# Rows normalised by GpSimd, one turn back, maxima turned by VectorE and an opening taken out of the loop, in a two-layer conditioned transformer

## The reference, cut to what matters

```
layer 0: sh_a,sc_a,gt_a,sh_m,sc_m,gt_m = split(silu(cond) @ Wada + bada)
  xm = (layernorm(x)*g1 + be1) * (1 + sc_a) + sh_a
  q,k,v = xm @ Wqkv;  P = softmax(causal(q @ k^T / 4))
  x = x + gt_a * ((P @ v) @ Wproj + bproj)
  xm = (layernorm(x)*g2 + be2) * (1 + sc_m) + sh_m
  x = x + gt_m * (gelu_exact(xm @ W1 + b1) @ W2 + b2)
layer 1: xm = layernorm(x) * (1 + scale1) + shift1        (scale, shift from cond)
  q,k,v = xm @ w^T + b;  P = softmax(q @ k^T / 4)          (no causal mask, a padding mask)
  x = x + (P @ v) @ wo^T + bo
  x = x + gelu_exact((layernorm(x)*(1+scale2)+shift2) @ w1^T + b1) @ w2^T + b2
```

## Time and profile before

| | before |
|---|---|
| runs, us | 1132.00, 1122.96, 1128.54 (median 1128.54) |
| the profiled execution, us | 1127.04 |
| its span, us | 1124.9 |
| PE, PEld | 1051.1 (93%), 905.2 (80%) |
| DVE | 828.6 (74%) |
| ACT | 592.0 (53%) |
| POOL | 347.9 (31%) |
| DMA packets | 50828, 81.46 MB |
| mean granted clock of TensorE | 0.968 |

### The profile page before, as it was taken

The page is one execution under the profiler, slowest core; times in us unless marked ns, Lnnn a source line. Parts: engine busy times, 40 slices in busy tenths (PEclk is TensorE's granted clock), DMA queues, the critical chain, the costliest instruction groups (busy, mean ns, idle before and its releaser), DMA issues.

```text
span 1124.9 us, 23896 instructions
## 1 busy us (share of the span) xinstructions
PE 1051.1 (93%) x8588; PEld 905.2 (80%) x8588; DVE 828.6 (74%) x2443; ACT 592.0 (53%) x1143; POOL 347.9 (31%) x333
## 2 busy tenths in 40 slices
PE   3879999999998899999998899999999888999998
PEld 3768888888886688998887787887888667889997
DVE  5478989999897476556638788898889845666553
ACT  1145666666665545433434677777777654344331
POOL 5112343343434544233411132323323343211111
PEclk9689999999999899999997899999999989999999
DMA  7565776757661020000068549466564400100001
GB/s 219 96 95 94 120 151 118 128 102 133 153 103 25 7 62 11 10 11 15 15 98 121 74 74 170 65 95 81 78 97 64 55 2 1 38 20 20 20 19 38
DMA packets 50828, 81.46 MB, mean 72 GB/s; under 512 B 8916, under 2 KB 23476, under 8 KB 49620
## 3 DMA queue, kind: packets, MB, share of 16 engines
q1 hardware_dynamic: 50232, 79.16, 40.3%
q10 hardware_dynamic: 480, 0.79, 0.6%
HBM read 22.64 MB, written 8.44 MB: 28 GB/s over the span
## 4 chain that ended last, share of the span: by engine, by line
PE 71%; DVE 8%; DMA 8%; SPq 5%; issue 4%; ACT 3%; POOL 1%; ACTq 0%; POOLq 0%; DVEq 0%
PE st_bank L576 14%; PE g_bank L576 12%; PE s_bank L576 8%; PE o_bank L576 8%; PE o_bank L664 7%; DMA k_stack<-qk_split 6%; SPq L433 4%; PE st_bank L643 3%; PE s_bank L626 3%; PE s_bank L630 3%; PE st_bank L649 3%; PE st_bank L645 2%; DVE maxima L1141 1%; PE g_bank L684 1%; PE st_bank L644 1%
## 5 line engine op out<-in xcount | busy, mean ns | idle before, releaser
L846 ACT ACTIVATE probs<-st_bank 128x384 f32<-128x384 f32 (+1 forms) x512 | 271.1, 545 | 194.1 <-PE st_bank L645 102.8
L1135 DVE CUSTOM_DVE_ANT_0 s_bank<-s_bank,tri_wide 128x128 f32<-128x128 f32 (+1 forms) x512 | 169.2, 382 | 25.6 <-PE s_bank L627 24.9
L1141 DVE TENSOR_REDUCE maxima<-s_bank 128x2 f32<-128x512 f32 x256 | 166.7, 675 | 24.7 <-PE s_bank L630 24.4
L933 ACT ACTIVATE probs<-st_bank,cols 128x512 f32<-128x512 f32 x112 | 77.2, 689 | 195.0 <-PE st_bank L576 185.1
L576 PE MATMUL st_bank<-qk_split,q_stack 128*128 128x512 f32 x696 | 166.5, 397 | 1.7 <-ACT probs L846 0.9
L576 PEld LDWEIGHTS st_bank<-qk_split,q_stack 128*128 128x128 f32 x696 | 129.3, 188 | 33.7 <-issue 1.9
L576 PE MATMUL g_bank<-xmT,wa 128*128 128x256 f32 x768 | 123.8, 301 | 4.8 <-POOL xmT L1358 4.8
L664 PE MATMUL o_bank<-probs,v_sb 128*32 128x256 f32 (+1 forms) x2048 | 126.1, 365 | 0.1
L630 PE MATMUL s_bank<-k_stack,q_stack 97*128 97x256 f32 x512 | 114.0, 307 | 12.2 <-DMA k_stack<-qk_split 6.9
L630 PEld LDWEIGHTS s_bank<-k_stack,q_stack 97*128 97x128 f32 x512 | 80.9, 196 | 41.1 <-issue 25.5
L649 PE MATMUL st_bank<-q_stack,k_stack 99*128 99x256 f32 x512 | 106.0, 291 | 6.6 <-ACT probs L846 3.3
(11 more groups left out here) (119 smaller groups left out, 2231.3 us busy)
## 6 DMA issues: line engine op xcount, KB each, us to landing
q_stack<-qk_split SPq DMA_DIRECT2D x192, 128.0 KB, 4.6
k_stack<-qk_split SPq DMA_DIRECT2D x186, 128.0 KB, 6.1
gate_rows<-gate_dram SPq DMA_DIRECT2D x32, 128.0 KB, 3.4
w_dram<-w_in SPq DMA_DIRECT2D x8, 512.0 KB, 7.2
wm_f32r<-w_dram SPq DMA_DIRECT2D x4, 1024.0 KB, 11.0
out<-x_sb SPq DMA_DIRECT2D x8, 512.0 KB, 2.9
x_sb<-x_in SPq DMA_DIRECT2D x4, 512.0 KB, 7.5
q_stack<-q_stack SPq DMA_DIRECT2D x4, 384.0 KB
```

The lines of the kernel that those rows point to most:

```text
L846: activation(probs[:, h % 8, 0:n], st_bank[h % 2][:, 0:n], ACT.Exp, scale=SCALE)\
L933: activation(h_of[b.const > 0][:, m % 2], h_bank(b, m)[:, :], ACT.Gelu, bias=cols[:, cb + m:cb + m + 1]).then_inc(m_gelu, 1)
L1135: last = v.tensor_tensor_reduce(out=bank[:, keys], in0=bank[:, keys], in1=tri_wide[:, T - (i + 1) * P:T], scale=1.0, scalar=LOWEST, op0=AL ...
L1141: v.reduce_max(maxima[:, gb.mod(2), :, slot], bank[:].rearrange("p (i n) -> p i n", n=T), AX.X).then_inc(max_done, 1)
```

## The change

1. From batch 2 of each layer on, in steady steps, POOL normalises the rows (two operations of 128x256) right after the inverse deviation; DVE did it at slot 9. DVE keeps the batches that open a layer.
2. The two scaling operations on DVE move from slots 0 and 7 to 4 and 8; the two turns back of 128x256 (slots 2, 8) become one of 128x512 at slot 9; ACT's high part of `attnT` moves from slot 9 to 10, the output projection from slots 12 and 14 to 13 and 15; POOL makes the low part in two operations of 128x256 where it was one of 128x512.
3. The turned maxima come from one DVE operation (a turn of 32x32 blocks over 128x64) at the end of the step that makes them. PE's two transposes, ACT's copy and their waits are gone. SP moves the maxima with four DMAs of 8 KB, whose pieces are 128 bytes, where it were two of 16 KB.
4. In layer 0, SP's wait for the added x and the load of the gate rows stand behind the restacks of q and k, where they stood ahead of both.
5. Layer 0's first two batches are opened ahead of the loop, which starts at t = 2. The block of conditioning matmuls is spread over the slots of step 2, one piece to a slot, behind that slot's scores; they go into `o_bank` instead of `s_bank[2]`. ACT issues the restack of k for the first two batches, not only for the first; v of batch 1 is made in step 2.

```diff
-SLOT = {"q": (0, 1), "negmaxT": 1, "k": (3, 5), "v": (6, 7), "xT": 12, "proj": (12, 14)}
-TURN, SCALED, TURN_BACK, ATTN_HIGH, PROJ_OUT = (14, 6), (0, 7), (2, 8), 9, 15
+SLOT = {"q": (0, 1), "k": (3, 5), "v": (6, 7), "xT": 12, "proj": (13, 15)}
+TURN, SCALED, TURN_BACK, ATTN_HIGH, PROJ_OUT = (14, 6), (4, 8), 9, 10, 15
-        negmaxT = sb("negmaxT", [32, T], f32r)
+        negmaxT = sb("negmaxT", [P, NT, 32])
...  (SP, step)
-                    when(negmaxT_copied, g.count(1, 1))
-                    for e in range(2):
-                        sp.dma_start(q_stack[ROW_MAX + e:ROW_MAX + e + 1, stack_of(g)].bitcast(fp32),
-                                     negmaxT[H * e:H * (e + 1)].bitcast(fp32)).then_inc(max_loaded[g.mod(2)], 16)
-                    if layer == 0:
-                        when(x_added, c.count(1, -1))
-                        load_gates(c, 0)
+                    when(negmax_turned, g.count(1, 1))
+                    rows = q_stack[ROW_MAX:ROW_MAX + 2, stack_of(g)].bitcast(fp32)\
+                        .rearrange("e s (i b n) -> e s i b n", i=NT, n=32)
+                    for blk in range(P // 32):
+                        sp.dma_start(rows[:, :, :, blk], negmaxT[32 * blk:32 * (blk + 1)])\
+                            .then_inc(max_loaded[g.mod(2)], 16)
...
+                if layer == 0 and c.within(B):
+                    if c.const == 0:
+                        store_tables()
+                    when(x_added, c.count(1, -1))
+                    load_gates(c, 0)
...  (PE, step)
-                    if s == SLOT["negmaxT"] and c.within(B):
-                        pe.wait_ge(negmax_ready, gc.count(1, 1))
-                        bank = take(layer, t, "negmaxT")
-                        for i in range(NT):
-                            src = negmax[:, gc.mod(2), i].bitcast(fp32).rearrange("p e s -> p (e s)")
-                            last = transpose(bank[0:32, i * P:(i + 1) * P], src, ident[:])
-                        last.then_inc(negmaxT_ready, 1)
...
+                    if layer == 0 and t.const == AHEAD and only is None:
+                        set_up(s)
...  (PE, the opening)
+            step(0, Step(0), "new")
+            pe.wait_ge(setup_done, 1)
+            step(0, Step(1), "project")
+            step(0, Step(1), "new")
+            step(0, Step(2), "project")
             for layer in range(LAYERS):
-                for t in steps(B, AHEAD * layer, 5):
+                for t in steps(B, AHEAD, 5):
                     step(layer, t)
-                    if layer == 0 and t.const == 1:
-                        set_up_columns()
-                        set_up_rows()
...  (DVE)
-                    if s == 9 and n.within(B):
-                        row_normalise(layer, n)
-                    if s in TURN_BACK and d.within(B):
-                        turn_back(gd, TURN_BACK.index(s))
+                    if s == TURN_BACK and d.within(B):
+                        turn_back(gd)
-                v.transpose(attnT_full[:, f], packed[:, f]).then_inc(attnT_ready, 1)
+                v.transpose(attnT_full.rearrange("p f n -> p (f n)"), packed[:].rearrange("p f n -> p (f n)"))\
+                    .then_inc(attnT_ready, 1)
...  (DVE, the end of negative_maximum)
+                v.transpose(negmaxT[:].rearrange("p i n -> p (i n)"),
+                            dst.bitcast(fp32).rearrange("p i e s -> p (i e s)")).then_inc(negmax_turned, 1)
...  (POOL)
-                g_.tensor_tensor(attnT[:, 1], attnT_full, attnT[:, 0], ALU.subtract).then_inc(attnT_lo, 1)
+                for f in range(NF):
+                    last = g_.tensor_tensor(attnT[:, 1, f], attnT_full[:, f], attnT[:, 0, f], ALU.subtract)
+                last.then_inc(attnT_lo, 1)
...
+            def row_normalise(layer, n):
+                gn = in_layer(layer, n)
+                wait(pool, xT_ready, gn.count(1, -1))
+                pool.wait_ge(rstd_ready, gn.count(1, 1))
+                rows = xrows(n, NT)
+                for i in range(NT):
+                    last = g_.tensor_scalar(xn[:, gn.mod(2), i], rows[:, i * D:(i + 1) * D], mv[:, gn.mod(2), i, 0:1],
+                                            rstd[:, gn.mod(2), i:i + 1], ALU.subtract, ALU.mult)
+                last.then_inc(xn_ready, 1)
+                if n.within(B) and t.const >= AHEAD:
+                    row_normalise(layer, n)
```

More of the change, by code:

```diff
@@ L341, in stack_of, with v_due @@
             return g.const % B % SBUFS
+        def v_due(layer, t, only):
+            if layer == 0 and t.const == AHEAD:
+                return only is None
+            return active(layer, t, only)[1].within(B)
         def active(layer, t, only):
@@ L350, in active @@
                 return off, a, off, off, off
-            if layer == 1 and t.const == AHEAD:
+            if t.const == AHEAD:
                 return n, off, b, c, d
@@ L704, in step @@
                                 last.then_inc(ready, 1)
-                    if s in SLOT["v"] and a.within(B):
+                    if s in SLOT["v"] and v_due(layer, t, only):
                         i = SLOT["v"].index(s)
+                        ga = in_layer(layer, t - 1)
                         if i == 0:
@@ L865, in step @@
                         exponentials(gc, s - LAG)
-                    if s == SLOT["negmaxT"] and c.within(B):
-                        act.wait_ge(negmaxT_ready, gc.count(1, 1))
-                        last_batch = gc - 1
-                        wait(act, max_loaded[last_batch.mod(2)], last_batch.half().count(32, 32)
-                             if c.const + layer else None)
-                        activation(negmaxT[:], g_bank[0][0:32, 0:T], ACT.Copy).then_inc(negmaxT_copied, 1)
                     if s == SLOT["q"][1] and a.within(B):
@@ L876, in step @@
                         high(k_ready, k_hi, k_stacked, g_bank[0], k_split, NF)
-                    if s == SLOT["k"][1] and a.within(B) and a.const + layer == 0:
+                    if s == SLOT["k"][1] and a.within(B) and layer == 0 and a.const < 2:
                         act.wait_ge(k_lo, ga.count(1, 1))
@@ L974, in mlp_step @@
                     step(1, Step(2), "project")
+            step(0, Step(0), "new")
+            step(0, Step(1), "project")
+            step(0, Step(1), "new")
+            step(0, Step(2), "project")
             for layer in range(LAYERS):
-                for t in steps(B, AHEAD * layer, 5):
+                for t in steps(B, AHEAD, 5):
                     if t.const == 3:
-                        act.wait_ge(setup_done, 3)
-                        act.wait_ge(mask_stored, 16)
                         wait(act, m_added, 2 * NCH * layer or None)
@@ L1119, in step @@
                 n, a, b, c, d = active(layer, t, only)
+                if layer == 0 and t.const == AHEAD:
+                    a = t - 1
                 gn, ga, gb, gc, gd = (in_layer(layer, s) for s in (n, a, b, c, d))
@@ L1191, in scale @@
                 dve.wait_ge(rsum_ready, g.count(NF, f + 1))
-                wait(dve, attnT_ready, g.count(NF, f - 1))
+                wait(dve, attnT_ready, g.count(1))
                 if g.const == 0:
@@ L1209, in negative_maximum @@
                 dve.wait_ge(max_done, g.count(H, H))
-                wait(dve, negmaxT_ready, g.count(1, -1))
+                wait(dve, negmax_turned, g.count(1))
                 v.tensor_scalar(dst[:, :, 0], m, -1.0, None, ALU.mult).then_inc(negmax_hi, 1)
@@ L1293, in _ @@
             for layer in range(LAYERS):
-                for t in steps(B, layer + 1, 5):
-                    if layer == 0 and t.const == 1:
-                        split_attention_weights()
+                if layer == 0:
+                    split_attention_weights()
+                    row_statistics(0, Step(1))
+                    row_normalise(0, Step(1))
+                    step(0, Step(1), "project")
+                    set_up_constants()
+                for t in steps(B, AHEAD, 5):
                     step(layer, t)
-                    if layer == 0 and t.const == 1:
+                    if layer == 0 and t.const == AHEAD:
                         set_up_columns()
@@ L1359, in modulated_low, with step @@
                     .then_inc(xmT_ready, 1)
-            def step(layer, t):
-                n, d = t, t - 4
+            def step(layer, t, only=None):
+                n, a, b, c, d = active(layer, t, only)
                 gd = in_layer(layer, d)
```

103 lines of the change are left out of this document (57 added, 46 removed).

## The result

The changed kernel takes 1163.4 us (median of four runs, 1158.54 to 1166.01) against 1128.35: ratio 1.031, interval 1.0273 to 1.0347. It is 3.1% slower where 1129, no change, was forecast, and outside the range (1106 to 1146).

The account below looks back on a forecast made before the run. PE was taken to bound the kernel (busy 49.02 of 50 us), DVE close behind. 1127.04 - 1.8 (opening) + 0.7 (layer 0 steps) - 1.1 (layer 1 steps) + 4.5 (last steps) = 1129.3, forecast 1129, range 1106 to 1146.

Parts of the forecast that it names:

- The DMAs of the maxima: Steady step: maxima split at 204.81, four DMAs issued by 207.5, landed at 209.2, before PE wants them at 209.80.
- The margin of 0.6 us: Maxima's DMAs land 0.6 us before PE's need, at 0.59 an issue; holds up to 0.75 us an issue.
- The slower rival: Maxima's DMAs come late at PE's first transposed scores of slot 4: 1.0 us in about 26 steps, 1155; chance 0.17.
- The projection: Steady steps: PE waits 0.67 (layer 0) or 0.61 (layer 1) for POOL's low part of attnT; 0.70 taken for both.
- The step without stalls: Distance between slot 12 transposes without stalls: 19.27 us before, less 0.22 for PE's two removed transposes.
- The first rival: Low part of attnT is in time: 24 steady steps lose 0.70 each, the tails 3; 1109.5; chance 0.32.
- The gate rows: Behind the restacks in layer 0: restacks begin up to 1 us sooner, so step-start stalls (0.45, 0.77) go.
- the forecast sign: In the changed profile, the stalls marked "issue" at the start of steps are gone.
- Normalising on POOL: DVE loses 2 x 0.775 us; POOL takes about 0.71 each, covered by its idle 5.04; worth nothing where PE bounds.
- The opening: Layer 0's start: step 2 ends at 61 to 63, gain 1.1; next three steps -0.7; -1.8 in all, bounds +3 and -10.
- The last steps: End of each layer: longer way to the low part costs +2.2 a layer, +4.5 in all, between 0 and 9.
- the prediction's own sign of having failed: Forecast fails if PE's steady-step waits sum to other than 0.7, or layers' last steps move over 5 us each.

Follow-up runs that it names:

- bias_waits: Changed kernel with one wait added: POOL's addition of the bias waits until both halves of the negated maxima are written; 1134.0 us, ratio 1.005.
- the pairs of the square: Four kernels compared: changed kernel 1163.4 us, maxima freed (bias_waits) 1134.0, projection freed (later_no_wait) 1141.1, both (projection_later) 1123.4.
- projection_later: bias_waits with scaling, turn back and high part of attnT one slot earlier (3 and 7, 8, 9), projection left at 13 and 15; 1123.4 us, ratio 0.9938.
- later_no_wait: projection_later without the wait of POOL's bias addition, so the changed kernel with scaling, turn back and high part a slot earlier; 1141.1 us, ratio 1.0119.
- opening_and_gates: Changed kernel with parts 1, 2 and 3 undone, leaving the opening ahead of the loop and gate rows behind the restacks; 1128.1 us, ratio 0.9982.
- earlier_and_waits: Changed kernel with scaling, turn back, high part and projection one slot earlier, and POOL's bias addition waiting for the negated maxima; 1125.3 us, ratio 0.9973.

## Why the prediction was wrong

- **The DMAs of the maxima**: this step failed, in its first term. "Split at 204.62 + 0.19" took the duration of the second maximum operation from the kernel before, where it began 0.26 ahead of POOL's addition. The change moved the projection to slot 15 and the two met. The operation took 1.27, so everything behind it was 1.1 late. bias_waits and the pairs of the square show it: 29 and 18 us. The trace of before held the warning: normalising took 775 ns a tile on DVE and 430 for the same shape in the MLP, and scaling 633 where it takes 430 in the changed kernel.

```profile
L1081 DVE TENSOR_SCALAR xn<-x_sb,mv_m,rstd_m 128x256 f32<-128x256 f32 x64 | 24.5, 430 | 0.0
```

  I counted the 775 as work that DVE would lose, did not ask what had made it long, and never asked which operation would be caught instead.
- The margin of 0.6 us was too large also without that. An issue took 0.68, not 0.59 (four in 2.73), below the point of 0.75 from which I said they decide; landing took 214.40 - 212.80 = 1.60, forecast 1.67. In bias_waits, with the operation at 0.19, PE still waits for these DMAs in 12 steps, by 0.18 in a steady one, where I had 0.6 to spare:

```profile
209.24 0.39 PE L655 MATMUL st_bank<-q_stack,k_stack 99*128 99x256 f32 x1 [0.18 <-DMA q_stack<-negmaxT]
```

  The slower rival had place and size nearly right (PE's first transposed scores, 1.0 us a step, 1155) and the cause wrong: that its number came close is luck. Four issues cost 2.73 where two cost 1.18, but pieces of 128 bytes do not land late here. The Trainium skill (DMA: Bandwidth & Descriptors, "Why small descriptors are slow (HBM only)") says so for transfers within SBUF, and these traces agree.
- **The projection**: a wait of 0.48 in layer 0 and 0.51 in layer 1 against 0.70; its mechanism was right. Taking it away was worth 22 and 11 us, against the 16.8 that the prediction gave to 24 steps.
- **What a stall costs beside its idle time** is open. PEld was idle 77.7 us at the three waits shown above where PE was idle 65.6, 0.2 us more at each of 61. If that were a price of its own, the maxima would have cost more than their waits; but from the changed kernel to bias_waits 33.3 us of such waits went and 29 us of time, and a step of layer 1 got shorter by 1.13 with 1.11 less idle time of PE.

The window of nine steps of the changed kernel, then that of eight steps of projection_later (us, busy and count of PE, PEld, DVE, ACT, POOL; clock, DMA share, GB/s):

```profile
699.34:890.07 190.73, 174.91 (x1622) 143.41 (x1621) 153.38 (x307) 124.20 (x244) 77.79 (x81) 1.00 0.61 89
```

```profile
697.00:853.23 156.23, 152.71 (x1442) 126.55 (x1441) 127.68 (x273) 112.51 (x217) 70.82 (x73) 1.00 0.60 84
```

PE is busy 19.43 us a step in the first and 19.09 in the second, for the same work; idle 1.76 and 0.44. In bias_waits it is busy 19.42, in later_no_wait 19.18: the difference goes with the projection's wait and hardly with that of the maxima. Why it is there, and why PE's busy time as a whole did not fall by the transposes removed, no run shows.

- **The step without stalls**, 19.27 - 0.22 = 19.05: close to PE's busy time a step in projection_later (19.09), but no kernel reached it as a mean period. With both waits gone a step is 19.5 to 19.6. In layer 0 of projection_later PE waits 7.9 us at 10 step starts, marked "issue"; in layer 1 its 0.44 of idle time a step stand mostly ahead of scores, for the maxima of L1149 and for the restack of k. The first rival, 1109.5, had assumed them absorbed; with its wait mended and the maxima freed, the time is 1123.4.
- **The gate rows**: this step failed too, at a smaller price. Behind the restacks they were to take the stalls at step starts away. The stalls went only where one of the two new waits stands (0.4 us left with both, 0.6 in bias_waits, 1.3 in later_no_wait), and with the same order of SP's queue they are 6.4 us in opening_and_gates and 7.9 in projection_later, against 4.7 before. That the changed kernel shows the forecast sign is luck.
- **Normalising on POOL** took 1.23 us a tile, not 0.71, and was hidden nonetheless.
- **The opening**: step 3 began at 60.0 (61 to 63 forecast, 63.58 before), 3.6 us sooner where the sum had 1.1; its transposes came 2.4 us sooner, and the granted clock was 0.50 while thin matmuls stood between the scores, as forecast:

```profile
50.00:55.00 5.00, 5.00 (x24) 4.39 (x24) 2.96 (x16) 0.32 (x1) 0.00 (x0) 0.50 1.12 199
```

- **The last steps**: from the last transposes of a steady step to the end of the span it was 265.1 before (from 859.79) and is 271.1 after (from 890.07), 6.0 more with both waits in it, against 2.2 forecast for a layer. In layer 0, from the last such transposes (318.45 before, 328.14 after) to the first of layer 1, it was 231.1 and is 239.6, 8.5 more, part of it at a clock of 0.96 against 0.98. More than 5 each was the prediction's own sign of having failed. In projection_later, without the two waits, they are 263.4 and 233.0.

Why freeing the maxima is worth 29 us in one pair and 18 in the other is not settled. In layer 1 the step shows the same, 1.13 and 0.79; in layer 0 the stalls at step starts stay at 0.6 us in the first pair (bias_waits) and come back, from 1.3 to 7.9, in the second. Nor was the meeting forced in the kernel before.

## What to carry to other kernels

When an edit shifts two engines against each other, list the operations of VectorE that read SBUF and those of POOL, and look which pairs now start together, and which of the two starts first: an operation's duration in the old trace is only valid for its old neighbours. Compare the mean of a group with the same shape elsewhere in the trace; a large difference (775 and 430 ns here) has a cause. A small operation at the head of a chain of DMAs deserves a clear place, and a wait on the engine with time to spare (here POOL) can buy it. And a stall that is gone from a profile may only be covered by a longer one; it comes back when that one is mended.

## What the runs showed of the hardware

- VectorE's operation with two SBUF inputs (L1220) that starts 0.01 to 0.06 us after POOL's addition does not slow down in proportion; it ends 0.04 to 0.06 after POOL's (1.27 to 1.33 us for 0.19 of work). The order of the two starts decides: one that starts 0.01 ahead of an operation of POOL keeps its time, in the changed kernel:

```profile
104.38 0.19 DVE L1220 SCALAR_TENSOR_TENSOR negmax<-maxima,negmax 128x32 fp32r<-128x32 f32 x1
104.39 1.33 POOL L1358 TENSOR_TENSOR y_sb<-y_sb,gate_rows 128x512 f32<-128x512 f32 x1
104.61 0.25 DVE L1226 STREAM_TRANSPOSE negmaxT<-negmax 128x64 f32<-128x64 f32 x1
```

- One of VectorE with a single tensor read from SBUF can be held as well. In the kernel before, the two operations that normalise a batch took 1.74 us beside POOL's low part of `attnT` (217.46 to 218.74) and ended 0.16 after it; clear of POOL (at 548.49) they took 0.73:

```profile
217.16 1.74 DVE L1081 TENSOR_SCALAR xn<-x_sb,mv,rstd 128x256 f32<-128x256 f32 x2
```

  The turn of the maxima, L1226, also reads one tensor from SBUF and was not held: in the rows above it starts 0.22 behind POOL's operation and takes 0.25, as it does clear of POOL (0.24 at 62.56 of bias_waits).
- One with a PSUM input beside the same addition kept its time, as the maxima L1149 did (0.69 us beside POOL's 1.28), in a step of earlier_and_waits:

```profile
746.25 1.28 POOL L1350 TENSOR_TENSOR y_sb<-y_sb,bias_rows 128x512 f32<-128x512 f32 x1 [1.23 <-ACT y_sb L904]
746.26 0.69 DVE L1149 TENSOR_REDUCE maxima<-s_bank 128x2 f32<-128x512 f32 x1
```

- The Trainium skill (GPSIMD Engine Reference, "8. Key points") names the contention with VectorE for instructions with two SBUF inputs or "in a 2-port perf mode". The traces agree for L1220, which has two SBUF inputs; in which mode the normalising ran, no row says.
- After four DMAs within SBUF whose pieces are 128 bytes, PE went on 1.60 us after the end of the last issue, as after the two of 16 KB before (1.67); an issue took 0.68 us against 0.59.
